# Grouping the score maxima by three instead of two, and where their masks are written, in an attention-plus-experts kernel

## The reference

```
xn  = layernorm(x)
q, k, v = split(xn @ w_qkv + b_qkv)            # 16 heads of 16
ctx = softmax(mask(q k^T / 4)) v               # heads 0-3: causal; heads 4-15: causal, at most 64 back
att = ctx @ w_out + b_out
Q, K = xn @ W_Q.T, xn @ W_K.T                  # and the same through W_inv
h   = (Q V_k) * cumsum_t(K W_k) * gate_k       # 8 experts of rank 64, forward and inverse
ffn = (sum_k h U_k + gate @ b) / n_valid, summed over both branches, @ W_O.T
out = x + att + ffn
```

## Time and profile before

| | |
|---|---|
| median of three runs | 1536.02 us |
| the profiled execution | 1539.46 us, of which 1537.7 us are the span from the first to the last instruction |
| PE busy / weight loads | 1441.1 us (94%) / 1072.7 us (70%) |
| DVE, ACT, POOL busy | 896.7, 842.4, 574.4 us |
| mean granted clock of PE | 0.990 |
| chain that ended last | PE 75%, DVE 10%, ACT 9%, waits for nothing seen ("issue") 5% |
| longest waits of DVE for PE at a peak | L1281: 54.6 us in all, L1288: 38.6 us |

### The profile page before, as it was taken

How to read it: one execution, slowest core, us unless ns; L and a number is a source line. 1 busy time by engine, 2 the same in 40 slices (tenths; PEclk the granted TensorE clock), 3 DMA queues, 4 the chain that set the end, 5 groups by cost and what they waited for, 6 DMA issues and landing times.

```text
span 1537.7 us, 36826 instructions
## 1 busy us (share of the span) xinstructions
PE 1441.1 (94%) x14977; PEld 1072.7 (70%) x14977; DVE 896.7 (58%) x1935; ACT 842.4 (55%) x1512; POOL 574.4 (37%) x663
## 2 busy tenths in 40 slices
PE   5999999999999999999999999999999999999997
PEld 4577685867758676676857777586776768677673
DVE  6665674566645675465745577355664557546451
ACT  3446556474665637565474645647365553746544
POOL 1044351443425333352424435143443524344341
PEclk9999999999999999999999999999999999999998
DMA  8422606253151625317153351615334062532600
GB/s 222 81 75 62 151 25 167 67 119 116 58 147 31 157 78 119 100 38 184 31 139 92 92 133 37 169 44 126 110 87 125 25 174 61 120 99 67 148 25 14
DMA packets 153788, 150.56 MB, mean 98 GB/s; under 512 B 28467, under 2 KB 136884, under 8 KB 153572
## 3 DMA queue, kind: packets, MB, share of 16 engines
q1 hardware_dynamic: 153620, 148.22, 37.2%
HBM read 106.98 MB, written 34.87 MB: 92 GB/s over the span
## 4 chain that ended last, share of the span: by engine, by line
PE 75%; DVE 10%; ACT 9%; issue 5%; POOL 1%; DMA 1%; SPq 0%; ACTq 0%; DVEq 0%; POOLq 0%
PE PS L656 36%; PE PS L777 11%; PE PS L811 4%; PE PS L928 3%; PE PS L797 3%; PE PS L897 3%; PE PS L879 3%; PE PS L865 3%; ACT HE L1112 2%; PE PS L983 2%; PE PS L909 2%; PE PS L841 2%; DVE prod L1361 2%; ACT HE L1104 2%; DVE PL L1380 1%
## 5 line engine op out<-in xcount | busy, mean ns | idle before, releaser
L1543 POOL TENSOR_TENSOR PL<-prod,PH 128x512 fp32r<-128x512 f32 x128 | 163.8, 1280 | 207.3 <-ACT PH L1074 207.3
L1538 POOL TENSOR_TENSOR prod<-prod,rest 128x512 f32<-128x512 f32 x96 | 123.2, 1285 | 273.9 <-ACT prod L1064 153.4
L656 PE MATMUL PS<-XH,WH 128*128 128x512 f32 x512 | 219.6, 429 | 4.5 <-DVE XL L1228 1.9
L1074 ACT ACTIVATE PH<-prod 128x512 fp32r<-128x512 f32 x128 | 80.9, 632 | 241.5 <-DVE prod L1361 241.5
L1288 DVE TENSOR_REDUCE block_peak<-PS 128x4 f32<-128x512 f32 x288 | 185.0, 685 | 38.6 <-PE PS L811 38.6
L656 PE MATMUL PS<-XL,WH 128*128 128x512 f32 x512 | 203.2, 397 | 0.0
L656 PE MATMUL PS<-XH,WL 128*128 128x512 f32 x512 | 203.1, 397 | 0.0
L1521 POOL TENSOR_SCALAR_AFFINE_SELECT HE<-HE 128x256 f32<-128x256 f32 x128 | 50.8, 409 | 349.6 <-ACT HE L1112 346.9
L1112 ACT ACTIVATE HE<-PS 128x512 f32<-128x512 f32 (+1 forms) x320 | 159.7, 552 | 27.2 <-PE PS L879 24.6
L1064 ACT ACTIVATE prod<-PS 128x512 f32<-128x512 f32 x128 | 76.2, 595 | 164.7 <-PE PS L656 164.7
L1281 DVE TENSOR_REDUCE peak<-PS 128x4 f32<-128x512 f32 x192 | 123.5, 684 | 54.7 <-PE PS L797 54.6
(11 more groups left out here) (196 smaller groups left out, 3174.4 us busy)
## 6 DMA issues: line engine op xcount, KB each, us to landing
parts_d<-area SPq DMA_DIRECT2D x32, 768.0 KB, 5.1
area<-parts_d SPq DMA_DIRECT2D x128, 192.0 KB, 8.4
rest<-weights_d SPq DMA_DIRECT2D x192, 128.0 KB, 2.9
area<-parts_d SPq DMA_DIRECT2D x32, 576.0 KB, 8.4
tok<-in_L_attn_x_dram SPq DMA_DIRECT2D x16, 512.0 KB, 6.3
xt<-in_L_attn_x_dram SPq DMA_DIRECT2D x16, 512.0 KB, 4.1
wide<-weights_d SPq DMA_DIRECT2D x64, 128.0 KB, 3.0
out_dram<-xt SPq DMA_DIRECT2D x16, 512.0 KB, 3.7
```

The costliest lines, as they stand in the source:

```text
L656: ins = e.matmul(ps, a, b, start=first and k == 0, stop=last and k == n - 1, skip_group_check=True)
L1074: e.activation(PH[:, h, :], prod[:, j % 3, :], ACT.Copy).then_inc(phi)
L1538: e.tensor_tensor(prod[:, j % 3, :], prod[:, j % 3, :], wide[j % WIDE], ALU.mult).then_inc(weighed)
L1543: e.tensor_tensor(PL[:, j % 2, :], prod[:, j % 3, :], PH[:, j % 2, :].bitcast(F32), ALU.subtract).then_inc(plo)
```

## The change

Three things change in the list. The peaks are woven in by groups of three (`PEAKS = 3`) instead of two. All the seeds of a group stand directly behind the group before it, instead of two peaks ahead of their own peak. And the first expert group and the first peak group of each chunk are run ahead, so that the weave spreads the remaining ones; `open` is joined with the `mix` behind it into one group. In the last chunk 4 expert groups instead of 3 go into the local phase.

```diff
+    PEAKS = 3
@@ expert_groups
-            if j == 1 and ch:
-                order.append([(add_open, ch)])
             if j:
-                order.append([(add_mix, ch, j - 1, part) for part in range(2)])
+                order.append([(add_open, ch)] if j == 1 and ch else [])
+                order[-1] += [(add_mix, ch, j - 1, part) for part in range(2)]
@@ peak_groups
+        masks = [[] for _ in order + gpeaks]
         for n, ((stage, *key),) in enumerate(order + gpeaks):
             if stage is add_lpeak and n > 2:
-                order[n - 2].append((add_seed, key[-1], "lpeak", *key[:-1]))
+                masks[n].append((add_seed, key[-1], "lpeak", *key[:-1]))
             elif stage is add_gpeak and key[2] == c * T + key[1]:
-                (order + gpeaks)[n - 2].append((add_seed, key[-1], "gpeak", *key[:-1]))
+                masks[n].append((add_seed, key[-1], "gpeak", *key[:-1]))
...
-        return [order[n] + (order[n + 1] if n + 1 < len(order) else []) for n in range(0, len(order), 2)]
+        blocks = range(0, len(order), PEAKS)
+        joined = lambda groups, n: [stage for group in groups[n:n + PEAKS] for stage in group]
+        return [joined(order, n) + joined(masks, n + PEAKS) for n in blocks]
@@ the loop over chunks
-        split = len(experts) if nxt else 18
-        weave(experts[:split], peaks)
+        split = len(experts) - (0 if nxt else 4)
+        run(experts[0] + peaks[0])
+        weave(experts[1:split], peaks[1:])
```

## The result

Over four runs each, the changed kernel took 1517.0 us (1516.08 to 1518.79) and the kernel before 1534.87 (1533.49 to 1538.45). The ratio is 0.987, with a 95% interval of 0.985 to 0.9889: 17.9 us less. The forecast was 1513 us, in a range of 1504 to 1524. The profiled execution took 1516.97 us (span 1515.3), where that of before took 1539.46 (span 1537.7). It lies at its median, that of before 3.4 to 4.6 us above its own, so the two profiles differ by 22.4 us and the medians by 17.9. Where the other 4.5 us are is a question of its own.

The account below looks back on a forecast made before the run. PE's list was taken to bound the peak phases; 11.2 us from 14 chunks, 4.3 from chunk 0 and 7.4 from the last chunk sum to 22.9 us, giving 1513 us against the median of 1536.02, range 1504 to 1524.

Parts of the forecast that it names:

- seven odd chunks, peak phase: Odd chunks' peak phases: fewer switches and old waits, some new waits; 40.4 us for 41.2, 0.8 us each.
- seven even chunks, peak phase: Even chunks' peak phases: fewer switches and waits, 0.25 us of new wait; 0.8 us saved in each, from 36.06.
- chunk 0, peak phase and clock behind it: End of chunk 0: PE's wait behind DVE's scaling goes, 2.9 us; full clock behind it, 1.4 us.
- last chunk, peak phase: Last chunk: `c` of j = 6 leaves the peak phase and waits at its start go; 34.9 instead of 37.37 us.
- last chunk, local phase: Last chunk's local phase: waits, slow clock and a missing filler go, a `c` comes in; 23.21 to 19.3 us.
- last chunk, global phase: Last chunk's global phase: its clock of 0.82 may rise if PE idles less ahead; 1.0 us taken of at most 2.5.
- the switches stay: Rival: the 0.10 us around a block comes from bank or operands, not the switch; 1523 us, 0.20 shared with two others.
- (a): New wait in odd chunks: PE's `rows`, behind the third global peak, waits for DVE's reductions and `found`; 0.75 us each.
- (b): New wait, once per odd chunk: a diagonal third peak's seed needs the preceding block's third bank; 0.4 us.
- (d): New wait in even chunks: `found` ahead of DVE's last product delays the last PL and first local masking; 0.25 us.
- No bank is free: Slower rival: blocks of three take all banks, PE waits for DVE's reductions; 1549 us, or 1531 at half; chance 0.06.
- ACT is held: Rival: ACT's nine seeds come 0.3 us later each and PE waits; 10 us back, 1523; 0.20 shared with two others.

Follow-up runs that it names:

- repeated pair: Kernel before and changed kernel, both unchanged, run and profiled again: medians 1536.49 us and 1516.77 us, spans 1532.9 and 1515.6 us.
- experiments 3 to 5: On the changed kernel: 3, old weave, 1516.91 us; 4, `rows` behind the sixth global peak, 1509.42; 5, as 4 plus diagonal global peak first in its block, 1505.03.
- Experiment 2: Changed kernel with the seeds two peaks ahead of their own peak, as in the kernel before: 1587.33 us in its one run.
- experiment 5: Changed kernel with `rows` behind the sixth global peak instead of the third and the diagonal global peak first in its block: 1505.03 us, ratio 0.9794.
- experiment 9: Experiment 5's kernel with the products of j = 6 and 7 one local group later in the last local phase: 1506.1 us, ratio 0.9791.
- experiment 1: Changed kernel with blocks of two peaks again (PEAKS = 2), all else as changed: 1532.01 us, ratio 0.9966.

## Why the prediction was right, and where it was not

| term | forecast, us | first pair of profiles | repeated pair |
|---|---|---|---|
| seven odd chunks, peak phase | 5.6 | 5.7 | 5.6 |
| seven even chunks, peak phase | 5.6 | 7.7 | 7.7 |
| chunk 0, peak phase and clock behind it | 4.3 | 3.65 | 3.4 |
| last chunk, peak phase | 2.5 | 2.58 | 2.57 |
| last chunk, local phase | 3.9 | 0.69 | -0.88 |
| last chunk, global phase | 1.0 | 2.2 | 0.0 |
| all else | 0 | -0.1 | -1.1 |
| span | 22.9 | 22.4 | 17.3 |

The -1.1 is mostly that chunk 0 began 1.5 us later in that execution of the changed kernel, at 85.54 us for 84.02, with a mean clock of 0.86 from 25 to 50 us where the other had 0.93.

*Blocks.* The switching is of the switch, not of the bank or the operands: a third peak adds 0.22 us and saves one whole change, as forecast (0.79 for 0.80, 0.65 for 0.65), and fp32 groups with no block beside them take 1.40 us. The first rival, "the switches stay", falls with it. The global block's switch was put at 0.06 us without a reason for that value; it is 0.09 to 0.1, and the prediction's own rows had it (1.48 us for the mix behind the block, 1.40 for a clean group).

*Odd chunks* came out at 40.39 us for 40.4, and experiments 3 to 5 show that the parts were right as well: (a) 0.83 for 0.75, (b) 0.44 for 0.4. With both causes gone, an odd phase takes 39.12 us.

*Even chunks* gained 1.05 us (chunk 12, which had taken 36.41, gained 1.40), not 0.8. The term that failed is (d): the 0.25 us for a late PL did not come in the even chunks. The local phase starts at once and takes 25.45 to 25.48 us in most of them, for 25.40 to 25.44 before. The list alone had given 35.0.

*No bank is free* and *ACT is held*, the rivals by which time comes back: the trace shows neither. In chunk 9 PE waits 0.2 us for a bank at one block, and the seeds cost 0.37 us of idle weights at one. The rule of the Trainium skill (Perfetto Trace Analysis, "Optimizing Tensor Performance", Matmuls) on rotating banks so that emptying overlaps with matmuls held only in part here: three banks fill in 0.65 to 0.79 us, and the 1.4 us or more of expert matmuls behind them are the cover. Experiment 2 is what the slower rival would look like, and its cause is ACT's order and not the number of banks.

*Chunk 0* lost its wait, as forecast. The phase came out 0.3 to 0.5 us longer than the 37.57 I had and the clock part 1.04 for 1.4.

*The last local phase* is the mis-sized term: 19.3 us forecast, 22.53 measured, 22.88 in the repeat. The sum itself was wrong: 23.21 - 2.5 - 2 + 1.5 is 20.2, and with up to 0.9 for POOL's work in front of masks 20.2 to 21.1, not 19.3. I took 2.5 us of the 2.92 of waits at its start for gained, and I did not follow ACT: with a fourth group there, the product of j = 6 also stands among the local groups, and its rounding holds the exponentials behind it. At full clock this phase takes 21.33 us (experiment 5, with the same list for it); experiment 9 took the hold away and it took 19.17. So the forecast's 19.3 is nearly what the phase takes without the hold, and that is luck. The other 1.2 us of the 22.53 go with the clock: a stretch of 3.4 us at the lower clock fell into this phase in both profiles of the changed kernel. In the first:

```profile
1465.50:1468.90 3.40, 3.40 (x22) 2.49 (x22) 0.54 (x1) 0.24 (x1) 0.58 (x1) 0.50 0.04 8
```

*The clock terms.* I read the clock of the last phases, 0.85 and 0.82, as a property of the kernel before, and priced a rise. In its second profile the same phases have 0.92 and 0.96. And I carried the 3.4 us by which that profile lay above the median over to the changed kernel, whose profile lies at its median. It was the clock of that execution: mean 0.990, where eight later runs of that kernel have 0.990 to 0.996, the two ends at 1541.57 and at 1534.65 us. So the forecast of 22.9 us matched the 22.4 of the first profiles partly by luck: the gain is 17.9 to 21.0 us by medians and 18.4 by the phases of the repeated pair (its first six rows). In that pair the even chunks gave 2.1 more than forecast and the last chunk 5.7 less. With either of these two errors alone the median would still have come into the range.

## What to carry to other kernels

Where one engine's list is the bound and its groups are of different kinds, count the changes of kind first: here a block of local peaks between fp32 groups cost 0.3 us beyond its own work and one of global peaks 0.1, and blocks of three instead of two, with the waits that they covered, gave 15 of the 17.9 us. When blocks grow, go through every stage that hangs on the n-th member of a block (masks, a transfer behind the third peak, the peak that needs its mask last): moving three of them was worth 70, 7.6 and 4.4 us by medians (the last across two chips; by the peak phases alone the last two are 6 and 4). And take a second profile before a stretch with a lowered clock is priced as the kernel's own.

## What the runs showed of the hardware

*GpSimd holds VectorE up.* The first step of `found` converts 128x48 numbers and takes 0.19 us at 900.90 in the changed kernel, but 0.77 before. For 128x16 numbers it took 1.17 in chunk 0 of the changed kernel. The two long ones fell under a subtraction of POOL. In the kernel before, the step took 0.189 to 0.191 us in all eight even chunks and 0.757 to 0.767 in seven of the eight odd ones; in the changed kernel it took 0.19 in all sixteen. DVE in chunk 0 of the changed kernel, then POOL there, then POOL in chunk 9 before, beside the earlier trace rows:

```profile
119.94 1.17 DVE L1307 TENSOR_SCALAR peak_t_global<-peak 128x16 bf16<-128x16 f32 x1
```

```profile
119.80 1.29 POOL L1547 TENSOR_TENSOR PL<-prod,PH 128x512 fp32r<-128x512 f32 x1 [2.46 <-ACT PH L1078]
```

```profile
912.78 1.28 POOL L1543 TENSOR_TENSOR PL<-prod,PH 128x512 fp32r<-128x512 f32 x1 [1.72 <-ACT PH L1074]
```

POOL ends at 121.09 and DVE at 121.11; POOL at 914.06 and DVE at 914.11. The Trainium skill (SBUF — State Buffer, "Who interferes with whom") says that the two share one pair of ports as an exclusive lock, and that a `tensor_scalar` can contend; these rows agree, with ends 0.02 and 0.05 us apart. It matters wherever `found` is waited for, and I had not priced it.

*The spread of the runs goes with the clock.* In the ten runs of experiment 1 the fastest (1528.38 us) had a mean clock of 0.999 and the slowest (1535.28) 0.994. In part the stretches at the lower level stay in place: one near 30 to 33 us and one in the last local phase stood in both profiles of the kernel before and in both of the changed kernel, and the one behind chunk 0's wait in both of the kernel before. Their length moved (the first 6.8 and 3.4 us in the two profiles of the kernel before, the last local phase's 6.8 and 3.4), and others came in one profile only, as the one of 6.8 us from 1504.8 on in the last global phase of the kernel before.
